# Two layers on one core: in layer 2, two of eight B products per group move to TensorE, and the chains of later chunks stand earlier in the program

## What is computed

```python
def _branch(x, conv_w, conv_b, W_xproj, W_dt, dt_bias, A_log, D):   # x: 3136 tokens x 384 channels
    xc = silu(conv_b + sum(xp[:, k:k + L, :] * conv_w[:, k] for k in range(4)))
    dbl = xc @ W_xproj.T
    dt = softplus(dbl[..., :12] @ W_dt.T + dt_bias)
    Bc, Cc = dbl[..., 12:28], dbl[..., 28:]
    A = -exp(A_log)
    # for each token, for 384 channels x 16 states:
    #   h = h * exp(dt * A) + (dt * x) * B ;  y = sum over states of h * C
    return selective_scan(xc, dt, Bc, Cc, A, D)
y = (y_f + y_b) * silu(z);  out = y @ W_out.T + b_out
```

## Time and profile before

| | us |
|---|---|
| median of 3 runs | 20762.58 |
| lowest, highest | 20758.69, 20782.99 |
| the profiled execution | 20745.35 |
| its span (first to last instruction) | 20743.6 |
| mean granted TensorE clock | 0.844 |

### The profile page before, as it was taken

The page is one execution under the profiler, slowest core; times in us unless marked ns, Lnnn a source line. Parts: engine busy times, 40 slices in busy tenths (PEclk is TensorE's granted clock), DMA queues, the critical chain, the costliest instruction groups (busy, mean ns, idle before and its releaser), DMA issues. The chain is left out here.

```text
span 20743.6 us, 188446 instructions
## 1 busy us (share of the span) xinstructions
PE 16102.5 (78%) x45152; PEld 5519.4 (27%) x45152; DVE 17255.4 (83%) x13583; ACT 13201.7 (64%) x33157; POOL 16916.4 (82%) x11028
## 2 busy tenths in 40 slices
PE   7777777777777777777777777777777777777777
PEld 2222222222222222222222222222222222222222
DVE  7888978889787897878878789787887878878788
ACT  5666656666565665656656566565665656666566
POOL 6878968789687896878968789687896978969689
PEclk8888888888888888888888888888888888888888
DMA  2423424234242342423424234242342423424243
GB/s 71 106 61 100 110 61 108 63 96 109 62 108 63 98 107 62 107 63 96 109 62 107 63 97 107 62 107 64 98 106 62 110 63 100 102 62 110 63 102 101
...
## 3 DMA queue, kind: packets, MB, share of 16 engines
...
## 5 line engine op out<-in xcount | busy, mean ns | idle before, releaser
L1151 DVE TENSOR_TENSOR_SCAN arena<-ps,arena 128x897 f32<-128x897 f32 x5376 | 10982.2, 2065 | 2194.7 <-issue 889.4
L1354 POOL TENSOR_TENSOR arena<-arena 128x896 f32<-128x896 f32 x5376 | 9414.5, 1766 | 428.3 <-DVE arena L1151 386.1
L1285 ACT ACTIVATE ps<-arena,A 128x448 f32<-128x448 f32 x10752 | 6390.3, 627 | 3539.1 <-DVE arena L1151 3426.3
L1057 PE MATMUL ps<-arena,rep 128*64 128x448 f32 x21504 | 5831.6, 673 | 1846.0 <-POOL arena L1354 1842.3
L1346 POOL TENSOR_TENSOR arena<-arena 128x896 f32<-128x896 f32 x2688 | 4761.3, 1772 | 1494.2 <-DMA arena<-arena 1494.2
L1057 PEld LDWEIGHTS ps<-arena,rep 128*64 128x64 f32 x21504 | 1533.7, 160 | 5661.2 <-POOL arena L1354 2884.0
L1140 DVE TENSOR_TENSOR arena<-ps,arena 128x896 f32<-128x896 f32 x2688 | 2864.2, 1066 | 131.3 <-PE ps L977 114.2
L1010 PE MATMUL ps<-arena,diag 128*128 128x448 f32 x5248 | 2308.8, 586 | 270.4 <-DVE arena L1114 227.4
L1010 PEld LDWEIGHTS ps<-arena,diag 128*128 128x128 f32 x5248 | 1040.1, 205 | 1563.1 <-issue 1160.6
L1022 PE MATMUL ps<-arena,wdt 13*128 13x448 f32 x1344 | 848.2, 731 | 641.0 <-DVE arena L1120 561.5
L1049 PE MATMUL ps<-arena,skipd 128*128 128x448 f32 x1344 | 832.5, 707 | 395.2 <-DVE arena L1127 266.6
...
## 6 DMA issues: line engine op xcount, KB each, us to landing
...
x_projected<-arena SPq DMA_DIRECT2D x112, 672.0 KB, 3.5
y_forward<-arena SPq DMA_DIRECT2D x112, 672.0 KB, 3.3
arena<-x_projected SPq DMA_DIRECT2D x112, 672.0 KB, 5.7
arena<-y_forward SPq DMA_DIRECT2D x112, 672.0 KB, 4.3
...
x_normed<-arena SPq DMA_DIRECT2D x112, 336.0 KB, 2.8
```

Source lines behind the costliest of these rows:

```text
L1057: m = e.matmul(ps[64 * h:64 * h + 64, YBANK, 0:T], rep[:, 0:64], pr[:, (q - 1 + h) % NPR, a * T:a * T + T], start=False, stop=p == NP - 1 ...
L1151: e.tensor_tensor_scan(rev(hh[:, q % NH, 0:W2], s), rev(decays(q)[:, 0:W2], s), rev(bb[:, q % NB, 0:W2], s), car[:, 2 * k + p % 2, n:n + 1 ...
L1285: e.activation(two(decays(q))[:, a, :], dt2[:, r % NR2, p % 2, :], ACT.Exp, scale=Am[s][:, 2 * k + p % 2, n:n + 1]).then_inc(c_ex, 1)
L1354: e.tensor_tensor(pr[:, q % NPR, :].rearrange("p (a b) -> p a b", a=2), two(hh[:, q % NH, :]), cr[:, p - p % 2:p - p % 2 + 2, :], ALU.mult ...
```

## The change

1. Of the eight units of a group, three products are made by POOL (p = 0, 2, 4), three by DVE (p = 1, 3, 5) and two by PE (p = 6, 7); before it was four and four.
2. For PE's products du is transposed (`dT`: four PE transposes of 112 tokens per group, then one ACT copy `dS` into `duT`, 112 partitions). The four B rows of p = 6, 7 become diagonals: `zw` writes them one value at a time into a DRAM tensor cleared once at the start, `zl` loads it back as `bz`, 112x112 blocks with B on the diagonal. A product is sixteen matmuls of 112 columns (duT block times diagonal block) into the PSUM pair that holds the decays of other units, and one matmul of one column (the carried state at the seam between the two runs). The decays of such a unit go to `bb` in SBUF, and the scan takes its two inputs the other way round.
3. PE makes `product(g + 1)` at the head of step g. It waits for scan g - 1, which frees the PSUM pair.
4. The chain of chunks i > 1 starts 2.5 units earlier. On SP, `dd` of group r stands no earlier than half a unit ahead of the start of group r - 2; `bl` has three pairs in place of four. Work banks are given by a rule on when they come free.

```diff
-ON_VECTOR = [[0, 1, 0, 1, 0, 1, 0, 1]] * 3
+POOL, DVE, PE = range(3)
+MAKER = [[POOL, DVE, POOL, DVE, POOL, DVE, PE, PE]] * 3
+TB, NTB = 112, 4
...
+        pe.append((o, "dT", i, e))
+        act.append((o + 0.8, "dS", i, e))
-        sp.extend([(t + 3.4, "dd", i, e), (t + 5, "ud", i, e)])
+        sp.extend([(max(t + 3.4, NP * (EJ * i + e - 2) - 0.5 if i else t), "dd", i, e), (t + 5, "ud", i, e)])
...
+        sp.append((t + 1.6, "zw", i, 0))
+        sp.append((max(t + 6.2, PER * i - 0.3), "zl", i, 0))
...
-        t = PER * (i - 1) if i else -60
+        t = PER * (i - 1) - 2.5 * (i > 1) if i else -60
...
-            for e, v in enumerate((1.3, 8.7, 10.7)):
+            for e, v in enumerate((1.3, 6.0, 10.7)):
...
+        def product(q):
+            r, i, k, p, s = pair(q)
+            b, h = DECAY[q % 2], p % 2
+            w.wait_ge(s_zl, 16 * (i + 1))
+            freed(w, "dT", i, k)
+            w.wait_ge(c_sc, q - 1)
...
+            e.matmul(ps[:, b, RS:RS + 1], ident[:, :], car[:, 2 * k + h, n:n + 1] if i % NC else zero[:, 0, 0:1],
+                     start=True, stop=True)
+            for a in range(2):
+                for n in range(NTB):
+                    for j in range(2):
+                        o = (RS - T) * (1 - a) + TB * n
+                        m = e.matmul(ps[64 * j:64 * j + 64, b + a, o:o + TB],
+                                     duT[:, r % NDR, n, 64 * h:64 * h + 64],
+                                     bz[:, n, (2 * j + a) * TB:(2 * j + a + 1) * TB], start=True, stop=True)
+            m.then_inc(c_be, 1)
...
         for g in range(-2, Q + LAG):
+            if 0 <= g + 1 < Q and maker(g + 1) == PE:
+                product(g + 1)
...
+            if maker(q) == PE:
+                w.wait_ge(c_sc, q - NB + 1)
+                o = two(bb[:, q % NB, :])
+            else:
+                w.wait_ge(c_sc, q - 1)
+                o = two(decays(q))
+                if q > 1 and maker(q - 2) == PE:
+                    e.activation(ps[:, DECAY[q % 2], RS:RS + 1], zero[:, 0, 0:1], ACT.Copy).then_inc(c_rz, 1)
...
+            if name == "zw":
+                w.wait_ge(s_zl, 16 * i)
+                with nc.allow_non_contiguous_dma(reason="one value per row of a block"):
+                    e.dma_start(zrows, res[44:48, :]).then_inc(s_zw, 16)
+            if name == "zl":
+                w.wait_ge(s_zw, 16 * (i + 1))
+                w.wait_ge(c_be, NE[PER * i])
+                e.dma_start(bz[:, :, :], zblocks).then_inc(s_zl, 16)
```

More of the change, by code:

```diff
@@ L28, with maker @@
 W2 = 2 * T + 1
-ON_VECTOR = [[0, 1, 0, 1, 0, 1, 0, 1]] * 3
-NV = [0]
+POOL, DVE, PE = range(3)
+MAKER = [[POOL, DVE, POOL, DVE, POOL, DVE, PE, PE]] * 3
+def maker(q):
+    return MAKER[q // NP % EJ][q % NP]
+NG, NV, NE = [0], [0], [0]
 for _q in range(Q):
-    NV.append(NV[-1] + ON_VECTOR[_q // NP % EJ][_q % NP])
+    for _n, _k in ((NG, POOL), (NV, DVE), (NE, PE)):
+        _n.append(_n[-1] + (maker(_q) == _k))
+TB, NTB = 112, 4
+RS = 511
 AHEAD, LAG = 2, 2
@@ L40 @@
 NXC, NDT, NDU, NR2 = 5, 3, 3, 3
+NDR = 3
 DECAY, DUBANK, YBANK, WBANK = (0, 2), 4, 5, (6, 7)
@@ L94, in project @@
             r = PER * i - NP + 2 * G if i else -100
-            sp.append((max(r + 1, t + 2 + 4 * (G > 0 and not i)), "bl", i, G))
+            if G < 3:
+                sp.append((max(r + 1, t + 2 + 4 * (G > 0 and not i)), "bl", i, G))
             sp.append((max(r + 3, t + 2.1 + 4 * (not i)), "cl", i, G))
@@ L115, in side_schedule @@
             sp += [(t + 5, "nw", i, 0), (t + 8, "xw", i, 0)]
-            for e, (u, v) in enumerate(((4.2, 6.4), (4.3, 7.4), (6.2, 11))):
+            for e, (u, v) in enumerate(((4.2, 6.4), (4.3, 8.6 if i > 1 else 7.4), (6.2, 11))):
                 pe.append((t + u, "x", i, e))
@@ L145, in side_schedule @@
     plans = [sorted(p, key=lambda a: a[0]) for p in (pe, act, dve, pool, sp)]
-    jobs, used = {}, {}
+    jobs, used, until = {}, {}, {}
+    last = dict(n1="nc", n2="nr", x="xe", cv="xc", xp="p1", t="td", z="z4", o="ou", dT="dS")
+    read = {(name, i, e): t for p in plans[1:4] for t, name, i, e in p}
+    release = {(name, i, e): read.get((last.get(name), i, e)) for _, name, i, e in plans[0]}
     for k, (t, name, i, e) in enumerate(a for a in plans[0] if a[1] != "dp"):
         banks = WBANK if t >= -10 else [*WBANK, 0, 1, 2, 3]
-        b = banks[k % len(banks)]
+        b = banks[k % len(banks)] if t < -10 else min(banks, key=lambda n: until.get(n, -99))
+        until[b] = release[name, i, e]
         jobs[name, i, e] = (k, b, used.get(b, 0))
@@ L252, in _ @@
             e.dma_start(xd[NC][:, :, 0:3], zero[:, :, :]).then_inc(s_wd, 16)
+            e.dma_start(zblocks,
+                        arena[0:TB, 0:NTB * T].rearrange("p (k c) -> p k c", k=NTB)).then_inc(s_wq, 16)
             for k, s in enumerate((1, 0)):
@@ L872, in build @@
     du2 = take(NR2, T, phase=0)
+    duT = take(NDR, NTB, 128, parts=TB)
+    bz = take(NTB, 4 * TB, parts=TB)
     res = take(T)
-    br = take(NP, T, phase=2)
+    br = take(NP - 2, T, phase=2)
     cr = take(NP, T, phase=2)
@@ L943, in product_done @@
     def product_done(w, q):
-        if ON_VECTOR[q // NP % EJ][q % NP]:
+        if maker(q) == DVE:
             w.wait_ge(c_bv, NV[q + 1])
+        elif maker(q) == POOL:
+            w.wait_ge(c_bp, NG[q + 1])
         else:
-            w.wait_ge(c_bp, q + 1 - NV[q + 1])
+            w.wait_ge(c_be, NE[q + 1])
     def y_free(w, r):
@@ L1157, in layer1_vector @@
                 scan(g)
-            if g + AHEAD < Q and ON_VECTOR[(g + AHEAD) // NP % EJ][(g + AHEAD) % NP]:
+            if g + AHEAD < Q and maker(g + AHEAD) == DVE:
                 product(g + AHEAD)
@@ L1291, in reset @@
             w.wait_ge(c_sc, q - NB + 1)
-            if i % NC:
+            given = i % NC and maker(q) != PE
+            if given:
                 w.wait_ge(c_ca, q - PER + 1)
-            e.activation(bb[:, q % NB, T:T1], car[:, 2 * k + p % 2, n:n + 1] if i % NC else zero[:, 0, 0:1],
+            e.activation(bb[:, q % NB, T:T1], car[:, 2 * k + p % 2, n:n + 1] if given else zero[:, 0, 0:1],
                          ACT.Copy).then_inc(c_rs, 1)
@@ L1360, in layer1_pool @@
                 output(g - 1)
-            if g + AHEAD < Q and not ON_VECTOR[(g + AHEAD) // NP % EJ][(g + AHEAD) % NP]:
+            if g + AHEAD < Q and maker(g + AHEAD) == POOL:
                 product(g + AHEAD)
```

65 lines of the change are left out of this document (50 added, 15 removed).

## The result

The changed kernel takes 21542 us (median of 4 runs, 21530 to 21557) against 20773 of the kernel before on the same chip: ratio 1.0371, 95% interval 1.0353 to 1.0388. It is 3.7% slower, where 20200 was predicted, with a range from 19400 to 21150. The profiled execution took 21543.8 us.

A forecast was written before the change was run, and what follows sets the result against it. POOL was taken as the bound, DVE right behind. DVE's remaining work plus hand-over, boundary, clock and other stalls gave chunks of 71.6 us forward and 73.3 backward, -560 us in all: 20,200 us, range 19,400 to 21,150.

The forecast's parts named there:

- The boundary: POOL's wait for a DMA once a chunk, 5.4 to 5.8 us, was to go but for 0.5 us.
- POOL and DVE: Each loses three products a chunk, 5.3 us of POOL and 3.2 of DVE, leaving DVE as the floor.
- A product: Sixteen matmuls plus a one-column matmul on PE: 1.9 us at 2.4 GHz, 3.7 at 1.2.
- rival 4: PE's weight loads are not hidden behind running matmuls, so a product costs 2.75 us: 21,340 us, chance 0.06.
- Diagonals: Writing 1792 single values and reading 800 KB back per chunk is hidden, except 3 us at an image's start.
- The clock: PE's granted clock rises to near 0.92; 1 us a chunk charged for what stays at the low clock.
- What waits for it: Scan 7 waits for PE's serial work after scan 4, stalling DVE 1.4 us plus side steps per group.
- Product 6 starts when scan 4 ends: In each group PE may begin product 6 once scan 4 is over; scan 7 follows 5.5 us plus side steps later.
- It runs at the full clock: Between scans 4 and 7, products were priced at 1.9 us each and the sum over states at 1.7.
- Only DVE waits for PE: The hand-over term priced DVE's stalls; other forward stalls got 3 us, since PE and ACT stay crowded.
- Rival 3: PE is the bound: with the clock still mixed, 2.0 us more per group, 21,300 us, chance 0.12.
- Rival 5: The boundary's wait stays, or another DMA wait (dt's or the B rows') replaces it: 21,200 us, chance 0.07.

The follow-up runs named there:

- experiment 13: Changed kernel with the first convolution of forward chunks i > 1 moved on PE from ahead of product 6 to between products 6 and 7: 21912.6 us.
- Experiment 6: Changed kernel with twelve added zero-weight matmuls on PE ahead of the wait for the scan at product 14 of each chunk: 21397.6 us.
- experiments 8: Changed kernel with PE's sum over states of units 2 and 3 of each group moved behind product 7: 21592.6 us.
- 9: Changed kernel with PE's side steps (projection, backward transposes, gate, normalisation) moved later, behind product 7: 21655.3 us.
- 12: Changed kernel with ACT's copy of the transposed du one unit later in ACT's order: 21771.7 us.
- 10: Changed kernel with the projection's matmuls (chunks i > 1) later on PE, and the ACT and SP steps that hang on them moved too: 21186.3 us.
- experiment 4: Changed kernel with four of the sixteen matmuls of each PE product, the rest left out: 19933.3 us.
- experiment 5: Changed kernel with only unit 6's product on PE, a quarter of it multiplied, and unit 7's made by DVE: 19908.1 us.

## Why the prediction was wrong

The account of the launch: 20761 - 1318 (the plan) + 131 (help work) + 1003 (product 6 of each group) + 965 (product 7) = 21542. Each term is the difference of two kernels in a row, so that the sum comes out proves nothing; what it shows is the size of each part.

**Right.** *The boundary*: 0.6 and 0.4 us a chunk are left, 0.5 was taken. *POOL and DVE*: busy for 62.6 and 61.9 us forward, 63.4 and 64.5 backward, where 61.8, 61.6, 62.5 and 63.7 were said. *A product*: 1.75 + 0.2 us at the full clock, as taken. *Weight loads*: 1.54 us of them lie inside the 1.75 us of matmuls, so rival 4 falls. The Trainium skill's rule would keep them apart, and the measurement decides against it (TensorE: Matmul & The Clock Gate, Part 3, "What overlaps and what doesn't"). *Diagonals*: hidden but for 79 us (48 were added). *The clock*: 0.89 to 0.93 in the chunks for 0.92.

**Wrong: the term "What waits for it".** It said 8.0 gross, 5.5 net forward, and 8.9 gross, 7.6 net backward. The scans fed by PE wait for 12.3 and 11.8 us a chunk: 6.8 and 4.2 us more. All the rest of DVE's idle time came out near the sum's other terms: forward (395.3 - 309.7 - 61.4) / 5 = 4.8 us for 4.5, backward (392.7 - 322.3 - 59.2) / 5 = 2.2 for 2.0. So this one term, with 0.8 us of DVE's backward work, is the miss: 7.5 and 5.2 us in chunks forecast at 71.6 and 73.3, times 7 and 16 some 1420 us; the miss is 21542 - 20200 = 1342.

What PE did between the end of scan 4 and the end of product 7, in us, means over the five chunks of all images, against the forecast:

| group | product 6's matmuls start | they take | until product 7's | these take | end of product 7 | forecast |
|---|---|---|---|---|---|---|
| forward 1 | 4.0 | 1.75 | 1.75 | 1.75 | 9.3 | 5.5 |
| forward 2 | 0.6 | 3.25 | 4.9 | 1.75 | 10.5 | 7.8 |
| forward 3 | 1.4 | 1.8 | 2.9 | 1.75 | 7.9 | 7.0 |
| backward 1 | 1.9 | 1.75 | 1.75 | 1.75 | 7.2 | 5.5 |
| backward 2 | 0.4 | 2.35 | 5.1 | 1.75 | 9.6 | 7.8 |
| backward 3 | 2.1 | 1.9 | 3.6 | 1.75 | 9.4 | 7.9 |

Product 7 is ready 7.4 us a chunk later than forecast forward (3.8 + 2.7 + 0.9) and 5.0 backward (1.7 + 1.8 + 1.5), and its scan starts 0.1 us behind it each time. Two assumptions of the term failed, and a third left something out.

1. *Product 6 starts when scan 4 ends.* This is the step that failed. It holds in the second group, where PE has been waiting for the scan (0.6 and 0.4 us are the matmul of one column). In the first and third, PE is still at its own program ahead of the product (a convolution, a sum over states), and the lateness, beyond the 0.2 us of the one-column matmul, adds up to 5.0 us a chunk forward and 3.6 backward. The forecast laid out what stands behind product 6 and nothing of what stands before it. Moving the convolution behind it did not help (experiment 13): PE's work is in order and had to go somewhere.
2. *It runs at the full clock.* In the second group PE has idled and then runs product 6, and most of the sum behind it, at the low clock: about 2.7 us a chunk forward and 1.8 backward. The 1 us charged for the clock stood in another term. Experiment 6 gave back 145 us of this; what a full mend would give wasn't measured.
3. *Only DVE waits for PE.* ACT waits too (1181.2 us at L1323 for the transposes), and DVE waits for ACT's decays, reset and carry. This is why steps are hard to move: experiments 8, 9, 12 and 13 each moved a step and came out 50 to 370 us slower, with the wait in another place. Only 10 gained by a move. It moved ACT's step with PE's; but 13 did so too and lost the most, so that alone doesn't make a move good.

**The rivals.** Rivals 3 and 4 (21,300 and 21,340) came nearest in time, but not by their mechanisms. Rival 4's unhidden weight loads aren't there. Rival 3 had the low clock cost 6 us a chunk on this path, in all groups; it cost 2.7 and 1.8, in the second group alone, and PE is busy for 68 of 79 us. PE isn't full, it is in series. Within a group, the path goes scan, product, sum and side steps, product, scan, and it grows with what a product lasts (1.2 of 1.3 us, experiment 4), whatever POOL and DVE shed beside it. The prediction saw this path and priced it from a start that PE had in one group of three. Rival 5 is false: 0.4 and 0.6 us are left at the boundary, and the waits of DVE's products for the B rows' DMAs are 121.8 us in the launch (17.1 before). Of what would show the forecast wrong, "scans wait for ACT more than for PE" held forward by the releasers' names (28.2 + 15.6 of 61.4 us); by the 0.10 us between product 7 and its scan it is PE all the same.

**The plan's gain was undersized**: 1318 us, where the boundary's whole wait was put at 1165, since the forward stalls beside the boundary went with it. That POOL at 67 to 68 us in a chunk of 68.4 to 68.8 can be fed without idling means that the kernel had 1318 us to win without PE. From there, the load shed by POOL and DVE could have given at most the way down to the busier of the two in the changed kernel: 68.8 - 62.6 = 6.2 us in a forward chunk, 68.4 - 64.5 = 3.9 in a backward one. The products gave back none of it.

**Open.** PE's products with the old start of the chains was not tried, so whether the two halves of the change help or hinder each other isn't known. Nor is it known how the 334 us that a quarter-length product 6 leaves (experiment 5) divide between that quarter, its waits and the PSUM pair's reuse. No order of PE's steps was found in which a product is free; that none exists isn't shown.
